# Attention and feed-forward layer on eight cores: the transposes that sum one tile's attention output are issued behind the output projection of the tile before it

## The chip, the cores and the metric

One Trainium2 chip, all eight NeuronCores, one launch. Each core computes 4096 of the 32768 rows on its own; no data goes between cores. The metric is device time in microseconds of the slowest core. Engines are named as in the profile: PE is TensorE (PEld its weight loads), DVE is VectorE, ACT is ScalarE, POOL is GpSimd, SP is SyncE, which here only issues DMAs.

## The reference, cut to what matters

The input is 4 x 8192 rows of 1024 float32. One layer is an attention in which each token attends only over its own 16 heads (a 16 x 16 score matrix for each token), and a gated feed-forward part with integer weights.

```python
Q = (x @ Wq.T).reshape(b, s, 16, 64)          # same for K, V; x is layer-normalised
scores = einsum('bshd,bstd->bsht', Q, K) / 8  # heads against heads, per token
attn = softmax(scores, axis=-1)
out = einsum('bsht,bstd->bshd', attn, V).reshape(b, s, 1024)
x = x + out @ Wfc.T
h = silu(ln(x) @ wg.T) * (ln(x) @ wu.T)       # hidden size 3072, weights int / 127
x = x + h @ wd.T
```

## The kernel before

The program has three stages with a barrier between them: the weights are transposed (to about 510 us), attention runs over 32 tiles of 128 tokens (about 480 to 2407 us), and the feed-forward part runs over 8 segments of 512 tokens (to the end). The change touches only the second stage.

A small class, `Sched`, keeps one list of instructions for each engine. Python code appends to the lists, so **the order of each engine's instructions is the order in which the code adds them**, and an engine runs its list strictly in that order. Waits are on counting semaphores.

The attention of a tile k is cut into pieces. In the main loop (step T from 0 to 35) each step adds one piece for each of several tiles:

- `front(T)` on DVE: four groups g, each a product of Q and K (L478, tile `gramB`, 128x4096), a folding add (L490, `gh`, 128x2048) and a sum (L502, `Ss`); then the maximum (L511) and the subtraction (L519, `Se`). ACT takes the exponential (L526).
- `a1(T-1)`: DVE normalises the scores (L535 to L554, tile `Aa`). Then POOL multiplies them with V in four groups g (L563, 128x4096 each), written to `avB[g % 2]`. So POOL can be two groups ahead of PE: group g waits (semaphore `aot`) until PE has read group g-2.
- `a2(T-2)`: PE adds up POOL's products with identity matmuls, 32 for each group, 128 in all, into `pOT` (L588). Each group waits for POOL's product of that group. ACT then copies `pOT` to the eight tiles `OT` (L604).
- `op2c(T-5)`: DVE applies the second layer norm (L383, `xn2m`), PE transposes it by eight matmuls (L671), ACT copies each (L680) and SP stores a finished block of four tiles.
- `op(T-3)`: PE multiplies `OT` with the output weights, twice eight matmuls (L622); DVE adds the residual to each half (L634, `x1p`); SP stores `x1p`; ACT sums values and squares (L345, L351).
- `op2m(T-4)`: four DVE instructions on 128x1 (L359, L362, L365, L367) and a logarithm and an exponential on ACT (L370, L375), for the second layer norm.
- `g_load(T+5)`, `g_a(T+4)`, `g_m(T+3)`: the load of a later tile, its sums on ACT and its own four DVE instructions of 128x1.
- `g_c(T+2)`: the first layer norm (L383, `xnm`), eight transposes (L425) with ACT copies (L433), and the 48 matmuls of Q, K and V (L452) with six copies by ACT (L466).

What sets the order around the change is only the order of these calls. POOL's list holds nothing but L563 in this stage, SP's the loads and stores. The two buffers of `avB` and the single `pOT` tie POOL and PE to each other:

```python
waits=[("amx", k + 1), ("aot", 4 * k + g - 1)], inc="apl")   # POOL, group g of tile k
w.append(("apl", 4 * k + g + 1))                              # PE, group g of tile k
```

Of the kernel before, what the change touches and what calls it, by code (L numbers as in the profile page):

```python
# [90 lines left out]
def build_program(taps=(), stop_after=None):  # L91
# [43 lines left out]
    with ExitStack() as TOP:  # L135
# [171 lines left out]
        with ExitStack() as ph:  # L307
# [268 lines left out]
            def back_a2(k):  # L576
                tt = k % 4
                for g in range(4):
                    for i in range(4):
                        for b in range(8):  # L580
                            w = []
                            if i == 0 and b == 0:
                                w.append(("apl", 4 * k + g + 1))
                                if g == 0:
                                    w.append(("aote", 8 * k))
                            S.add("tensor",
                                  lambda e, g=g, i=i, b=b:
                                  e.matmul(pOT[:, 128 * b:128 * (b + 1)],  # L588
                                           avB[g % 2][:, 1024 * i + 128 * b:
                                                       1024 * i + 128 * (b + 1)],  # L590
                                           ident[:],
                                           start=(g == 0 and i == 0
                                                  and b % 4 == 0),
                                           stop=(g == 3 and i == 3
                                                 and b % 4 == 3)),
                                  waits=w,
                                  inc=("aot" if (i == 3 and b == 7) else None))
                ev_w0 = [("aot", 4 * (k + 1))]
                if k - 4 >= 0:
                    ev_w0.append(("arp", 2 * (k - 4 + 1)))  # L600
                for b in range(8):
                    S.add("scalar",
                          lambda e, b=b, tt=tt:
                          e.copy(OT[b][:, tt * 128:(tt + 1) * 128],  # L604
                                 pOT[:, 128 * b:128 * (b + 1)]),
                          waits=(ev_w0 if b == 0 else []), inc="aote")
# [45 lines left out]
            def back_b2m(k):  # L652
                cap["l2m", k] = ln_mid(S, Lr2[k % 4], cap["l2a", k])
# [40 lines left out]
            def a1(k):  # L694
                if 0 <= k <= 31:
                    back_a(k)

            def a2(k):
                if 0 <= k <= 31:
                    back_a2(k)  # L700

            def op(k):
                if 0 <= k <= 31:
                    back_b(k)

            def op2m(k):
                if 0 <= k <= 31:
                    back_b2m(k)

            def op2c(k):  # L710
                if 0 <= k <= 31:
                    back_b2c(k)

            def g_load(k):
                if 5 <= k <= 31:
                    load_tile(k)

            def g_a(k):
                if 4 <= k <= 31:
                    ln1_a(k)  # L720

            def g_m(k):
                if 3 <= k <= 31:
                    ln1_m(k)

            def g_c(k):
                if 2 <= k <= 31:
                    ln1_c(k)
                    lnt(k)
                    proj(k)  # L730
# [11 lines left out]
            for T in range(36):  # L742
                if T <= 31:
                    front(T)
                a1(T - 1)
                a2(T - 2)
                op2c(T - 5)
                op(T - 3)
                op2m(T - 4)
                g_load(T + 5)  # L750
                g_a(T + 4)
                g_m(T + 3)
                g_c(T + 2)
# [175 lines left out]
```

How the kernel before makes its waits and increments, by code:

```python
                    def f(e):  # L71
                        for op in ops:
                            waits = list(op["waits"])
                            for tok in op["deps"]:
                                waits.append(selfcount[tok])
                            for (s, v) in waits:
                                key = (eng_name, s)
                                if v > 0 and hwm.get(key, 0) < v:
                                    e.wait_ge(sems[s], v)
                                    hwm[key] = v
                            ins = op["fn"](e)
                            if op["inc"] is not None:
                                ins.then_inc(sems[op["inc"]], op["incn"])
                            elif op["selfneed"]:
                                ins.then_inc(sems["sf" + eng_name], 1)
# [71 lines left out]
                    def f(e, k=k):  # L157
                        e.nop().then_inc(sems["ph"], 1)
                        e.wait_ge(sems["ph"], NENG * k)
# [7 lines left out]
                @blk.sync  # L167
                def _(sy):
                    t0 = cnt.get("tapd", 0)
                    add = [0]
                    def issue(dst, src):
                        sy.dma_start(dst, src).then_inc(sems["tapd"], 16)
                        add[0] += 16
                    for (_, fn) in todo:
                        fn(issue)
                    sy.wait_ge(sems["tapd"], t0 + add[0])
                    cnt["tapd"] = t0 + add[0]
```

## Time and profile before

| | us |
|---|---|
| median of the 2 runs shown (3659.9 and 3869.12) | 3764.51 |
| profiled execution, its own time | 3664.66 |
| its span, slowest core (core 0) | 3663.1 |
| spans of the eight cores | 3625.3 to 3663.1 |
| DVE busy | 1937.3 (53%) |
| PE busy | 2262.9 (62%) |
| POOL busy | 1138.4 (31%) |
| ACT busy | 682.4 (19%) |
| mean granted clock of TensorE, core 0 | 0.841 |

The span runs from the first to the last instruction of the slowest core. Busy shares are means over stages with different limits: in the attention stage DVE is the busiest engine, in the feed-forward stage PE is. A row of the timeline gives the start in us from the span's start, how long the instruction took in us, the engine, the line of the kernel, the operation with its output and inputs, and in square brackets the idle time in front of it with what ended it. An instruction that is held up after it was issued shows that as a longer duration, not as idle time.

### The profile page before, as it was taken

Reading aid. Unit: us, or ns where it says so; the run is one execution under the profiler, and the core shown is the slowest. Engines: PE = TensorE matmul, PEld = TensorE weight load, DVE = VectorE, ACT = ScalarE, POOL = GpSimd, SP = SyncE. Lnnn points to the kernel's source line nnn. Section 1 sums busy time; section 2 is a strip of 40 time slices with the busy share of each in tenths; the row PEclk is TensorE's granted clock in tenths of the full one; section 3 lists DMA queues with packets and bytes.
Section 4 is the critical chain, followed back from the end, with each engine's and each line's share of the span. In section 5 each row is a group of like instructions: output and inputs, shape, how many; then the busy total and the mean of one; then the engine's idle time right before and its main releaser. Section 6 shows DMA issues by size and latency. Waiting matters only on the chain. (4 is left out here: it accounts for less than half of the span.)

```text
span 3663.1 us, 38294 instructions; the slowest of 8 cores (3625.3 to 3663.1 us)
## 1 busy us (share of the span) xinstructions
PE 2262.9 (62%) x12192; PEld 1160.2 (32%) x12352; DVE 1937.3 (53%) x2305; ACT 682.4 (19%) x1691; POOL 1138.4 (31%) x447
## 2 busy tenths in 40 slices
PE   4433443554545555454555644468989889898897
PEld 2111112323333233333333333323434334343343
DVE  4433459988878787787878778511111111111111
ACT  0112231122222222122221211121101111011110
POOL 1000004546465554645446465601101111010110
PEclk9999996767777777777767766679999999999999
DMA  5445310000100101001010000034445444454443
GB/s 98 121 152 180 145 64 1 12 24 12 35 23 13 35 12 35 12 24 35 12 35 12 18 18 12 24 121 164 147 161 184 138 152 147 169 178 130 162 148 138
DMA packets 109631, 302.39 MB, mean 83 GB/s; under 512 B 13184, under 2 KB 29568, under 8 KB 108416
## 3 DMA queue, kind: packets, MB, share of 16 engines
q1 hardware_dynamic: 68736, 159.41, 13.4%
q0 software_dynamic: 32640, 121.65, 10.6%
q10 hardware_dynamic: 8064, 18.88, 1.3%
q8 instruction: 108, 1.77, 0.2%
q14 instruction: 83, 0.68, 0.1%
HBM read 247.46 MB, written 60.82 MB: 84 GB/s over the span
## 5 line engine op out<-in xcount | busy, mean ns | idle before, releaser
L563 POOL TENSOR_TENSOR avB<-Aa,Vs 128x4096 bf16<-128x4096 bf16 x128 | 971.3, 7608 | 1051.1 <-PE pOT L588 713.2
L588 PE MATMUL pOT<-ident,avB 128*128 128x128 bf16 x4096 | 344.9, 264 | 349.8 <-POOL avB L563 349.8
L834 DVE TENSOR_TENSOR hseg<-sg,pU 128x512 bf16<-128x512 bf16 x192 | 132.0, 688 | 620.4 <-PE pU L829 620.4
L588 PEld LDWEIGHTS pOT<-ident,avB 128*128 128x128 bf16 x4096 | 328.9, 121 | 368.9 <-issue 361.4
L815 PE MATMUL pG<-x2s,wgS 128*128 128x512 bf16 x1505 | 369.2, 387 | 44.2 <-DMA wgS<-d_wgT 40.6
L829 PE MATMUL pU<-x2s,wuS 128*128 128x512 bf16 x1505 | 366.8, 385 | 17.2 <-DMA wuS<-d_wuT 15.3
L270 PE MATMUL wps<-ident,wstg_b 128*128 128x128 bf16 x832 | 187.5, 265 | 285.8 <-ACT wstg_b L249 133.3
L861 PE MATMUL pD<-hseg,wdC 128*128 128x512 bf16 x1501 | 347.1, 386 | 18.5 <-DMA wdC<-d_wdT 14.6
L490 DVE TENSOR_TENSOR gh<-gramB 128x2048 bf16<-128x2048 bf16 x128 | 329.4, 2574 | 13.6 <-DVE gramB L478 0.5
L478 DVE TENSOR_TENSOR gramB<-Qs,Ks 128x4096 bf16<-128x4096 bf16 x128 | 319.4, 2495 | 25.5 <-ACT Vs L466 12.2
L804 POOL DMA_DIRECT2D wuS<-d_wuT x192 | 103.0, 537 | 727.3 <-PE pU L829 667.3
L502 DVE TENSOR_REDUCE Ss<-gh 128x64 f32<-128x2048 bf16 x128 | 292.6, 2286 | 13.2
L878 DVE TENSOR_TENSOR yst<-pT,x1s 128x128 f32<-128x128 f32 x256 | 63.6, 287 | 435.9 <-PE pT L871 435.6
L292 DVE CAST wpk<-wps 128x128 bf16<-128x128 f32 x576 | 143.0, 288 | 209.6 <-PE wps L270 207.8
L425 PE MATMUL pT<-ident,xnm 128*128 128x128 bf16 x256 | 53.1, 257 | 297.1 <-DVE xnm L383 211.6
L383 DVE TENSOR_SCALAR xn2m<-x1p,Lr 128x1024 bf16<-128x1024 f32 x32 | 222.7, 6958 | 12.9 <-ACT Lr L375 9.5
L820 ACT ACTIVATE sg<-pG 128x512 bf16<-128x512 f32 x192 | 114.6, 597 | 595.8 <-PE pG L815 595.7
L815 PEld LDWEIGHTS pG<-x2s,wgS 128*128 128x128 bf16 x1536 | 148.0, 99 | 236.5 <-issue 72.9
L829 PEld LDWEIGHTS pU<-x2s,wuS 128*128 128x128 bf16 x1536 | 151.4, 99 | 206.4 <-issue 33.2
L671 PE MATMUL pT<-ident,xn2m 128*128 128x128 bf16 x256 | 54.4, 271 | 259.1 <-DVE xn2m L383 223.6
L861 PEld LDWEIGHTS pD<-hseg,wdC 128*128 128x128 bf16 x1536 | 147.7, 99 | 196.1 <-issue 32.2
L270 PEld LDWEIGHTS wps<-ident,wstg_b 128*128 128x128 bf16 x832 | 86.6, 104 | 386.5 <-issue 354.6
(78 smaller groups left out, 2021.5 us busy)
## 6 DMA issues: line engine op xcount, KB each, us to landing
wuS<-d_wuT POOLq DMA_DIRECT2D x192, 256.0 KB, 3.2
wgS<-d_wgT SPq DMA_DIRECT2D x192, 256.0 KB, 2.7
wdC<-d_wdT POOLq DMA_DIRECT2D x64, 768.0 KB, 4.8
xcT<-x SPq DMA_DIRECT2D x32, 512.0 KB, 4.4
d_x<-x1p SPq DMA_DIRECT2D x32, 512.0 KB, 2.9
x1s<-d_x SPq DMA_DIRECT2D x8, 2048.0 KB, 13.7
y<-yst SPq DMA_DIRECT2D x32, 512.0 KB, 4.4
wstg_i<-wg SPq DMA_DIRECT2D x24, 512.0 KB, 3.6
```

The lines of the kernel that those rows point to most:

```text
L270: e.matmul(wps[b % 2][:, 0:128], wstg_b[j % 4][:, b * 128:(b + 1) * 128], ident[:], start=True, stop=True),
L292: e.tensor_copy(pdst(e), wps[b % 2][:, 0:128]),
L383: lambda e: e.tensor_scalar(out_fn(), xsrc_fn(), Lrt[:, 2:3], Lrt[:, 7:8], ALU.add, ALU.mult),
L478: e.tensor_tensor(gramB[g % 2][:].rearrange("p (t h d) -> p t h d", t=4, d=64), bass.AP(Qs[tt][:].tensor, Qs[tt][:].offset, [[1024, 128], ...
L490: e.tensor_tensor(gh1[:].rearrange("p (a b) -> p a b", b=32), bass.AP(gramB[g % 2][:].tensor, gramB[g % 2][:].offset, [[4096, 128], [64, 6 ...
L502: e.tensor_reduce(Ss[:, 64 * g:64 * (g + 1)] .rearrange("p (a b) -> p a b", b=1), gh1[:].rearrange("p (a b) -> p a b", b=32), AX.X, ALU.add),
L563: e.tensor_tensor(avB[g % 2][:].rearrange("p (t h d) -> p t h d", t=4, d=64), bass.AP(Aa[e4][:].tensor, Aa[e4][:].offset + 64 * g, [[256, ...
L588: e.matmul(pOT[:, 128 * b:128 * (b + 1)], avB[g % 2][:, 1024 * i + 128 * b: 1024 * i + 128 * (b + 1)], ident[:], start=(g == 0 and i == 0 ...
L815: e.matmul(pG[h % 2][:], wgS[h % 2][:, j * 128:(j + 1) * 128], x2buf[xp][j][:], start=(j == 0), stop=(j == 7)),
L829: e.matmul(pU[h % 2][:], wuS[h % 2][:, j * 128:(j + 1) * 128], x2buf[xp][j][:], start=(j == 0), stop=(j == 7)),
L834: lambda e, h=h: e.tensor_mul(hseg[h][:], sg[h % 2][:], pU[h % 2][:]),
L861: e.matmul(pD[c % 2][:], wdC[c % 2][:, k * 128:(k + 1) * 128], hseg[k][:], start=(k == 0), stop=(k == 23)),
```

## The change

Within each step of the main loop the call `a2(T - 2)` moves from ahead of `op2c(T - 5)` and `op(T - 3)` to behind them. Nothing else changes: the same instructions, buffers and semaphores.

```diff
                 a1(T - 1)
-                a2(T - 2)
                 op2c(T - 5)
                 op(T - 3)
+                a2(T - 2)
                 op2m(T - 4)
                 g_load(T + 5)
                 g_a(T + 4)
                 g_m(T + 3)
                 g_c(T + 2)
```

PE's list changes. Before, one step in the steady part, from the last matmuls of `g_c` to the first transposes of the next `g_c`:

```order
 L452 MATMUL pB<-WvJ,xnT 128x512 x8
 L588 MATMUL pOT<-ident,avB 128x128 x128
 L671 MATMUL pT<-ident,xn2m 128x128 x8
 L622 MATMUL pA<-WfJ,OT 128x512 x8
 L622 MATMUL pB<-WfJ,OT 128x512 x8
 L425 MATMUL pT<-ident,xnm 128x128 x8
```

The same place of PE's list after the change:

```order
 L452 MATMUL pB<-WvJ,xnT 128x512 x8
 L671 MATMUL pT<-ident,xn2m 128x128 x8
 L622 MATMUL pA<-WfJ,OT 128x512 x8
 L622 MATMUL pB<-WfJ,OT 128x512 x8
 L588 MATMUL pOT<-ident,avB 128x128 x128
 L425 MATMUL pT<-ident,xnm 128x128 x8
```

The 128 matmuls of `pOT` (L588) now stand behind the transposes of `xn2m` (L671) and the output projection (L622), and directly ahead of the transposes of `xnm` (L425).

ACT's list, one step in the steady part, as a difference (L604 is the copy of `pOT`, `Lr_1` a small tile of the second layer norm):

```order
 L466 CAST Vs<-pB 128x512
 L526 ACTIVATE Se<-Se 128x256
-L604 CAST OT<-pOT 128x128 x8
 L680 CAST xn2s<-pT 128x128 x8
 L345 ACTIVATE sqd,Lr_2<-x1p 128x1024
 L351 ACTIVATE sqd,Lr_2<-x1p 128x1024
+L604 CAST OT<-pOT 128x128 x8
 L370 ACTIVATE Lr_1<-Lr_1,c_eps 128x1
 L375 ACTIVATE Lr_1<-Lr_1 128x1
```

The eight copies of `pOT` follow the matmuls: they now stand behind the copies of `xn2s` and the two sums over `x1p`, and ahead of everything that belongs to `op2m`, `g_a`, `g_m` and `g_c`. The lists of DVE, POOL and SP are the same as before.

## Rows read from the trace of the kernel before

**Rows 1.** Stages: us, busy us (and count) of each engine, PE clock, DMA.

```profile
1200.00:1760.00 560.00, 304.56 (x1996) 181.00 (x2016) 451.30 (x311) 139.95 (x421) 287.23 (x39) 0.73 0.07 25
2560.00:3663.00 1103.00, 955.65 (x4230) 417.89 (x4316) 174.19 (x404) 134.23 (x226) 119.78 (x225) 0.98 0.46 155
```

**Rows 2.** Timeline of DVE through one step of the steady part.

```profile
1500.29 0.69 DVE L634 TENSOR_TENSOR x1p<-pB,xcT 128x512 f32<-128x512 f32 x1 [1.18 <-PE pB L622]
...
1504.11 2.29 DVE L478 TENSOR_TENSOR gramB<-Qs,Ks 128x4096 bf16<-128x4096 bf16 x1
...
1525.20 7.86 DVE L490 TENSOR_TENSOR gh<-gramB 128x2048 bf16<-128x2048 bf16 x1
...
1536.24 3.99 DVE L519 TENSOR_TENSOR Se<-Ss,Sm 128x256 bf16<-128x256 f32 x1
...
1542.60 7.67 DVE L383 TENSOR_SCALAR xn2m<-x1p,Lr 128x1024 bf16<-128x1024 f32 x1
1556.76 0.69 DVE L634 TENSOR_TENSOR x1p<-pA,xcT 128x512 f32<-128x512 f32 x1 [6.49 <-PE pA L622]
1558.48 0.69 DVE L634 TENSOR_TENSOR x1p<-pB,xcT 128x512 f32<-128x512 f32 x1 [1.03 <-PE pB L622]
```

**Rows 3.** Timeline of POOL through the same step (two instructions in each row).

```profile
1523.40 16.55 POOL L563 TENSOR_TENSOR avB<-Aa,Vs 128x4096 bf16<-128x4096 bf16 x2 [24.63 <-PE pOT L588]
1542.69 14.46 POOL L563 TENSOR_TENSOR avB<-Aa,Vs 128x4096 bf16<-128x4096 bf16 x2 [2.74 <-DVE Aa L554]
```

**Rows 4.** Timeline of PE through the same step.

```profile
1521.30 3.74 PE L588 MATMUL pOT<-ident,avB 128*128 128x128 bf16 x64
...
1540.10 3.28 PE L588 MATMUL pOT<-ident,avB 128*128 128x128 bf16 x32 [4.39 <-POOL avB L563]
1550.41 0.37 PE L671 MATMUL pT<-ident,xn2m 128*128 128x128 bf16 x2 [7.04 <-DVE xn2m L383]
```

**Rows 5.** DVE groups by line, whole span: count, duration ns min/median/max.

```profile
L490 DVE TENSOR_TENSOR gh<-gramB x128: 1224/1226/7865, 514.2 to 2293.7; 128x2048 bf16<-128x2048 bf16 x128
L519 DVE TENSOR_TENSOR Se<-Ss,Sm x32: 425/3990/3996, 537.0 to 2298.1; 128x256 bf16<-128x256 f32 x32
L383 DVE TENSOR_SCALAR xn2m<-x1p,Lr x32: 811/7673/7675, 786.9 to 2402.8; 128x1024 bf16<-128x1024 f32 x32
L502 DVE TENSOR_REDUCE Ss<-gh x128: 2285/2286/2289, 515.6 to 2295.0; 128x64 f32<-128x2048 bf16 x128
```

**Rows 6.** Timeline of DVE in step T = 3.

```profile
680.98 5.42 DVE L365 TENSOR_TENSOR Lr<-Lr 128x1 f32<-128x1 f32 x1
686.50 6.88 DVE L367 TENSOR_TENSOR Lr<-Lr 128x1 f32<-128x1 f32 x1
```

**Rows 7.** Timeline of POOL in step T = 3.

```profile
679.36 14.02 POOL L563 TENSOR_TENSOR avB<-Aa,Vs 128x4096 bf16<-128x4096 bf16 x2 [7.15 <-DVE Aa L554]
```

**Rows 8.** Timeline of DVE where step T = 30 ends.

```profile
2257.57 0.69 DVE L634 TENSOR_TENSOR x1p<-pB,xcT 128x512 f32<-128x512 f32 x1 [1.66 <-PE pB L622]
...
2259.41 9.16 DVE L478 TENSOR_TENSOR gramB<-Qs,Ks 128x4096 bf16<-128x4096 bf16 x1
```

**Rows 9.** Timeline of PE, then of POOL, at the same place.

```profile
2257.29 3.74 PE L588 MATMUL pOT<-ident,avB 128*128 128x128 bf16 x64
...
2259.39 16.06 POOL L563 TENSOR_TENSOR avB<-Aa,Vs 128x4096 bf16<-128x4096 bf16 x2 [3.79 <-PE pOT L588]
```

**Rows 10.** Timeline of DVE: second residual add of steps 5 and 31.

```profile
803.43 0.69 DVE L634 TENSOR_TENSOR x1p<-pB,xcT 128x512 f32<-128x512 f32 x1 [1.71 <-PE pB L622]
...
2316.62 0.69 DVE L634 TENSOR_TENSOR x1p<-pB,xcT 128x512 f32<-128x512 f32 x1 [0.97 <-PE pB L622]
```

**Rows 11.** Timeline of all engines in the stage's last steps.

```profile
2384.05 0.81 DVE L383 TENSOR_SCALAR xn2m<-x1p,Lr 128x1024 bf16<-128x1024 f32 x1 [2.02 <-ACT Lr L375]
...
2394.01 0.69 DVE L634 TENSOR_TENSOR x1p<-pB,xcT 128x512 f32<-128x512 f32 x1 [1.75 <-PE pB L622]
...
2406.57 0.43 ACT L680 CAST xn2s<-pT 128x128 bf16<-128x128 f32 x2 [0.33 <-PE pT L671]
```

## The prediction, made before the changed kernel ran

> **What bounds the kernel now.** I read the stage table first. The change lies in the attention stage, where DVE is busy 451 of 560 us and PE only 305, at a granted clock of 0.73; in the feed-forward stage PE is busy 956 of 1103 us at 0.98, and that stage holds none of the moved instructions, so I leave it as it is [rows 1]. So DVE's list sets the pace of the stage, and the question is what DVE does in its 58 us per step.
>
> The timeline of DVE through one step, from one second residual add to the next, is 1500.29 to 1558.48 us: 58.2 us [rows 2]. Two things in it are not DVE's own work:
>
> - It stands idle twice for the output projection, 6.49 and 1.03 us, 7.5 in all [rows 2].
> - Three of its instructions are far longer than the shortest of their kind: L490 7.86 instead of 1.22, L519 3.99 instead of 0.42, L383 7.67 instead of 0.81 [rows 2, 5]. That is 6.6 + 3.6 + 6.9 = 17.1 us.
>
> POOL's timeline beside it says why. POOL multiplies at 1523.40 to 1539.95 and at 1542.69 to 1557.15, two instructions each time [rows 3]. L490 starts at 1525.20, behind the start of a POOL instruction, and ends about when that one does; L519 and L383 are caught in the same way. The sum L502 never stretches: its 128 executions lie between 2285 and 2289 ns, many beside POOL [rows 5]. Even instructions of one element are caught: L365 takes 5.42 and L367 6.88 us while POOL runs its two from 679.36 on [rows 6, 7]. So in this kernel a POOL product of some 7.0 us (14.02 for two) shuts out these elementwise instructions of DVE until it ends; then DVE gets one through, and then POOL's next one runs. The sums pass, and so do the adds from PSUM (L634, 0.69 us at 1556.76, where POOL is still busy). The Trainium skill says as much for part of these (GPSIMD Engine Reference, Key points: GpSimd shares its SBUF interfaces with VectorE and contends with its two-input and two-port instructions); the stretched L490 and L365 have two inputs, so the trace agrees.
>
> The own work of DVE is then 58.2 - 7.5 - 17.1 = 33.6 us per step, and the step is decided by **where POOL's four products (28 us) fall in DVE's list**.
>
> **The change part by part.**
>
> *PE's order.* What could be gained is the wait of the adds for the output projection, now 7.5 us. But PE was not late because of L588: its last group starts at 1540.10 and takes 3.28, so it is over at 1543.4, and PE then idles 7.04 us for xn2m [rows 4]. From the end of xn2m (1550.27) to the end of the second add (1559.17) there are 8.9 us of transposes and projection, which the change leaves in a row. So the gain here is nothing in the steady part.
>
> *When POOL may start.* POOL's third group of a tile waits for PE to have read the first. Before, PE reads it at 1521.30, right behind the projections, in the middle of DVE's front; two groups run there, and the first two groups of the next tile run behind Aa at 1542.69, the second of them beside the 7.5 us in which DVE is idle anyway [rows 2 to 4]. That idle time is where POOL was free of charge. After the change PE comes to L588 only when the output projection is over, which is at the second add. The end of step 30 shows this meeting by chance, because PE was late there: L588 starts at 2257.29, the second add at 2257.57, POOL at 2259.39 [rows 8, 9]. So POOL's third group will start 1.8 us behind the start of the second add, or 1.0 us behind its end. By then Aa of the next tile is long made, and PE frees each buffer in 3.3 to 3.7 us, within the 7 us of the next product. **All four products will run back to back right behind the second add.**
>
> *The walk.* Let 0 be the end of the second add. DVE's list then holds eight instructions of one element, 0.26 us apart, of which the third, fourth, seventh and eighth have two inputs; then xnm at 2.1 and L478 at 3.0 (as 1500.99 to 1504.11 [rows 2]).
>
> - POOL's first, 1.0 to 8.0: L365 of the second group of four, issued at 1.6, is held to about 8.2. By the nearest row L365 loses 5.3 us issued later in a product; here 6.5.
> - POOL's second, to 15.1: L367 is held, 6.88 instead of 0.16 [rows 6]: 6.7.
> - POOL's third, to 22.1: xnm is held as xn2m is now, 7.67 instead of 0.81 [rows 5]: 6.9.
> - POOL's fourth, to 29.6: L478 is held, 9.16 instead of 2.29, as at 2259.41 [rows 2, 8]: 6.9.
>
> That is 27.0 us held instead of 17.1: +9.9 us a step. Nothing else in the step is then held, since POOL is through by 30 us; xn2m is free, but the 7.5 us idle stay behind it. The step becomes 33.6 + 7.5 + 27.0 = 68.1 us.
>
> *Other engines.* PE's list: behind L588 stand the transposes of xnm and Q, K, V. L588 ends about 19 us into the step, xnm is there at 23, and the 48 matmuls end near 39; the front that needs them starts more than 25 us later. Covered; without that cover it would cost 20 us a step. ACT: the eight copies of pOT now hold L370 and L375, g_a and the copies of g_c till about 21 us; their users on DVE come at 58 us or in the next step. SP's and POOL's lists don't change; SP's loads wait for the adds of tiles seven back, so they don't matter.
>
> *The clock.* PE will idle some 20 us ahead of the transposes, not 7. Where they start behind other work, end of xn2m to end of the second add is 8.9 us; in the stage's last steps, with few matmuls around, it is 2384.86 to 2394.70, 9.8 us [rows 2, 11]. I take the upper one: +0.9 a step, bounds 0 and 0.9.
>
> *How many steps.* From step 5 to step 31 the second add goes from 803.43 to 2316.62, 26 steps of 58.2 us [rows 10]. Each gets +9.9 + 0.9: 26 x 10.8 = +281.
>
> *The start.* In steps 3 and 4 there is no op2c, so the projection goes ahead without a wait: step 4 loses an idle time that I take as half of the steady 7.5 us, 4. In step 5 POOL's last two groups move to behind the add, so this step is held by no product: about -17. Small shifts in steps 3 and 4 give 2 more: together -23.
>
> *The tail.* From the second add of step 31 (over at 2317.3) to the end of the stage (2407.0) it is 90 us [rows 10, 11]. After the change POOL has ten products left there instead of eight, at 7 us with PE's reads between the last of them, and each of PE's pieces waits its turn: my walk gives 111 us, +21 (bounds 0 and 40).
>
> Sum: 281 - 23 + 21 = +279, on the profiled execution's own 3664.7: **3944 us, 7.6% slower.** I say 3940. The median of the runs shown, 3764.5, is of two that lie 209 us apart; the profiled one agrees with the lower, and I add to that.
>
> **The rivals.**
>
> 1. *POOL's burst falls a little later.* If L588 starts later or on a slow clock, POOL's first product starts when L478 has begun. Then L490, L478, L490 and L478 are hit, and two of the four holds are cut by L502, which runs beside POOL (2.3 us each): about 22.6 us held, +5.5 and +0.9 a step. 26 x 6.4 = +166, with start and tail +164: 3829. For it: step 30 was only 1.0 us from there. Against it: the row of L588 has 64 matmuls in 3.74, fast, behind a projection [rows 9].
> 2. *No change.* The products slip into the idle time as now. For this POOL would have to start two of them 30 us later, with Aa ready; nothing holds it back. 3665.
> 3. *Faster: holds need a two-port mode.* If only xnm and xn2m could be held and the other three stretched kinds have another cause tied to the old places, a step would be 33.6 + 7.5 + 6.9 + 0.9 = 48.9, 9.3 less than now, over 26 steps -242: 3423. It decides from the point that no two-input instruction is held. Against it stand L365, L367 and L478, held in other places [rows 6, 8]. The Trainium skill speaks for it: Advanced Engine Details and Errata, VectorE Performance Modes, names only two-port instructions as those that GpSimd blocks. L490 and L365 say otherwise here.
> 4. *Much slower.* The Q, K, V path becomes late because ACT and PE stand behind L588. It needs 25 us that I don't see; +5 a step more would give 4070.
>
> **How the numbers follow.** Forecast 0.70, rival 1 0.15, rival 4 0.07, rival 2 0.05, rival 3 0.03. About 2% either way is what a measurement of this kernel tells from no change; faster 0.03, same 0.05, slower 0.92. The range goes from between rival 1 and the forecast to just short of rival 4, 3840 to 4050; its upper part also takes in that the runs shown scatter upwards.
>
> **What would show it.** Right: a DVE step of 68 us; L365, L367, xnm and the first L478 at 6.6 to 9.2 us each step, L490, L519 and xn2m back at 1.2, 0.42 and 0.81; POOL in one burst of four behind the second add; the adds still waiting 6 to 7 us for PE. Wrong: stretched instructions elsewhere, products beside DVE's idle time, or DVE idle ahead of L478 for ACT's copies of Q and K.

## The result, and the profile after

The changed kernel takes 1.069 times as long as the kernel before (95% interval 1.0647 to 1.0733): 3910 to 3941 us against 3657 to 3696. The profiled execution took 3913.5 us, against 3664.7 before, so +249; 3940 was forecast. Nearly every kernel here also had executions some 1 to 7% longer, with a lower TensorE clock on one die or both; all times and ratios below leave these out.

The stages of the changed kernel (core 5, its slowest; us, busy us of PE, PEld, DVE, ACT and POOL, clock, DMA share, GB/s):

```profile
1200.00:1760.00 560.00, 270.22 (x1732) 159.70 (x1732) 468.46 (x260) 118.12 (x362) 244.70 (x36) 0.68 0.06 19
2680.00:3780.00 1100.00, 971.07 (x4346) 421.67 (x4345) 175.03 (x397) 136.64 (x230) 122.26 (x229) 0.98 0.48 157
```

Against [rows 1], DVE is busier in the attention stage, 468 us instead of 451, although it got through fewer instructions, 260 instead of 311, and POOL did 36 products instead of 39. More busy and less done is the sign of an instruction that waits after it was issued. The feed-forward stage is as it was.

The timeline of DVE from one second add of the output projection on:

```profile
1598.53 0.69 DVE L634 TENSOR_TENSOR x1p<-pB,xcT 128x512 f32<-128x512 f32 x1 [1.85 <-PE pB L622]
...
1599.85 0.16 DVE L365 TENSOR_TENSOR Lr<-Lr 128x1 f32<-128x1 f32 x1
1600.12 0.16 DVE L367 TENSOR_TENSOR Lr<-Lr 128x1 f32<-128x1 f32 x1
1600.38 0.15 DVE L359 TENSOR_SCALAR Lr<-Lr 128x1 f32<-128x1 f32 x1
1600.64 0.15 DVE L362 TENSOR_SCALAR Lr<-Lr 128x1 f32<-128x1 f32 x1
1600.90 6.50 DVE L365 TENSOR_TENSOR Lr<-Lr 128x1 f32<-128x1 f32 x1
1607.51 6.88 DVE L367 TENSOR_TENSOR Lr<-Lr 128x1 f32<-128x1 f32 x1
1614.50 7.41 DVE L383 TENSOR_SCALAR xnm<-xcT,Lr 128x1024 bf16<-128x1024 f32 x1
1622.01 8.93 DVE L478 TENSOR_TENSOR gramB<-Qs,Ks 128x4096 bf16<-128x4096 bf16 x1
```

POOL in the same stretch:

```profile
1600.36 28.43 POOL L563 TENSOR_TENSOR avB<-Aa,Vs 128x4096 bf16<-128x4096 bf16 x4 [39.73 <-PE pOT L588]
```

And PE:

```profile
1589.38 0.37 PE L671 MATMUL pT<-ident,xn2m 128*128 128x128 bf16 x2 [18.40 <-DVE xn2m L383]
...
1592.24 3.57 PE L622 MATMUL pA<-WfJ,OT 128*128 128x512 bf16 x8
1595.61 2.82 PE L622 MATMUL pB<-WfJ,OT 128*128 128x512 bf16 x8
1598.26 3.74 PE L588 MATMUL pOT<-ident,avB 128*128 128x128 bf16 x64
```

Read them together. PE reaches L588 at 1598.26, at the second add (1598.53). The first 32 of these 64 matmuls free a buffer, and POOL starts at 1600.36, 1.1 us behind the end of the add. Its four products then run in one piece for 28.4 us, where before they came in two pairs [rows 3]. Each catches one instruction of DVE: a pair of instructions on a single element, 6.50 and 6.88 us long instead of 0.16, then xnm, then the first L478. The instructions that were held before are free now:

```profile
L490 DVE TENSOR_TENSOR gh<-gramB x128: 1224/1226/7864, 516.0 to 2523.3; 128x2048 bf16<-128x2048 bf16 x128
...
L519 DVE TENSOR_TENSOR Se<-Ss,Sm x32: 425/425/4032, 538.8 to 2527.7; 128x256 bf16<-128x256 f32 x32
...
L383 DVE TENSOR_SCALAR xnm<-xcT,Lr x32: 812/7412/7554, 495.2 to 2413.5; 128x1024 bf16<-128x1024 f32 x32
L383 DVE TENSOR_SCALAR xn2m<-x1p,Lr x32: 811/812/1504, 773.7 to 2652.4; 128x1024 bf16<-128x1024 f32 x32
```

These groups by line give minimum, median and maximum in ns. The median of L519 fell from 3990 to 425 and that of xn2m from 7673 to 812, while xnm rose to 7412; compare [rows 5].

Where the 249 us came from, by the second adds of steps 5 and 31 and the last copy of the stage:

```profile
783.19 0.69 DVE L634 TENSOR_TENSOR x1p<-pB,xcT 128x512 f32<-128x512 f32 x1 [1.42 <-PE pB L622]
...
2540.60 0.69 DVE L634 TENSOR_TENSOR x1p<-pB,xcT 128x512 f32<-128x512 f32 x1 [1.86 <-PE pB L622]
...
2656.10 0.54 ACT L680 CAST xn2s<-pT 128x128 bf16<-128x128 f32 x2 [0.23 <-PE pT L671]
```

Up to step 5 the changed kernel is 20.2 us ahead (783.2 against 803.4); over the next 26 steps it loses 244.2 (1757.4 us against 1513.2); behind step 31 it loses 25.7 more (115.3 against 89.7, from the add's end to the end of the stage). The sum, 249.7, is the whole difference of the two profiled executions (248.8), to within a microsecond.

For all kernels, the 26 steps from the second add of step 5 to that of step 31 split as follows. "Held" is the time by which DVE's instructions were longer than the shortest of their kind (0.16 us for L365 and L367 in either form), "idle" the gaps between them beyond the 0.1 us that lies between any two. Both are summed from the trace of the slowest core (for e5_split2 core 2, for e10_all_new_order core 5) and divided by 26; us per step:

| kernel | step | held | of it, mainly | idle |
|---|---|---|---|---|
| before | 58.2 | 17.2 | xn2m 6.9, L490 5.6, L519 3.3 | 7.7 |
| changed | 67.6 | 26.1 | L478 7.0, xnm 6.4, L367 6.2, L365 5.8 | 8.1 |
| e1_single | 64.9 | 23.3 | L478 10.9, L490 6.9, xnm 5.3 | 8.2 |
| e2_before4 | 58.5 | 17.6 | xn2m 6.9, L367 6.7, L365 4.0 | 7.6 |
| e3_after4 | 67.6 | 26.1 | as changed | 8.1 |
| e4_moved | 61.3 | 21.8 | L490 13.3, L478 8.5 | 6.3 |
| e5_split2 | 54.1 | 13.2 | xn2m 3.3, L490 3.2, L544 2.9, L541 2.2 | 7.5 |
| e6_small_idle | 55.0 | 16.6 | xn2m 6.9, L541 4.9, L519 3.5 | 5.1 |
| e8_old_late_pool | 67.1 | 26.1 | L367 12.9, L365 12.1 | 7.7 |
| e9_all | 52.4 | 13.7 | L383 4.5, L490 3.0, L544 2.9, L541 2.2 | 5.3 |
| e10_all_new_order | 53.8 | 15.7 | L490 12.8, L478 2.5 | 4.8 |
| e11_split4 | 53.0 | 8.8 | L383 1.9, L544, L547 and L554 1.5 each | 10.9 |

### The profile page after: what moved, and what is told of

Same layout as the page of the kernel before. It is cut to its first block and busy times, and to the rows that moved or that the text cites. A ratio compares the mean times of both kernels' runs of the same rounds, so it can differ in the third digit from the quotient of the medians.

```text
span 3911.9 us, 38454 instructions; the slowest of 8 cores (3883.2 to 3911.9 us)
## 1 busy us (share of the span) xinstructions
PE 2313.1 (59%) x12352; PEld 1166.9 (30%) x12352; DVE 2155.3 (55%) x2305; ACT 683.8 (17%) x1691; POOL 1085.5 (28%) x447
## 3 DMA queue, kind: packets, MB, share of 16 engines
q1 hardware_dynamic: 68736, 159.41, 12.8%
## 5 line engine op out<-in xcount | busy, mean ns | idle before, releaser
L563 POOL TENSOR_TENSOR avB<-Aa,Vs 128x4096 bf16<-128x4096 bf16 x128 | 918.3, 7204 | 1365.7 <-PE pOT L588 1130.5
L588 PE MATMUL pOT<-ident,avB 128*128 128x128 bf16 x4096 | 344.4, 263 | 293.0 <-POOL avB L563 293.0
L478 DVE TENSOR_TENSOR gramB<-Qs,Ks 128x4096 bf16<-128x4096 bf16 x128 | 480.4, 3753 | 27.0 <-ACT Vs L466 13.7
L588 PEld LDWEIGHTS pOT<-ident,avB 128*128 128x128 bf16 x4096 | 328.1, 121 | 312.2 <-issue 304.7
L671 PE MATMUL pT<-ident,xn2m 128*128 128x128 bf16 x256 | 55.4, 270 | 577.9 <-DVE xn2m L383 544.0
L861 PE MATMUL pD<-hseg,wdC 128*128 128x512 bf16 x1536 | 352.4, 387 | 18.6 <-DMA wdC<-d_wdT 17.2
L502 DVE TENSOR_REDUCE Ss<-gh 128x64 f32<-128x2048 bf16 x128 | 292.6, 2286 | 13.2
L671 PEld LDWEIGHTS pT<-ident,xn2m 128*128 128x128 bf16 x256 | 25.0, 105 | 616.9 <-issue 611.4
L425 PE MATMUL pT<-ident,xnm 128*128 128x128 bf16 x256 | 54.6, 265 | 252.3 <-DVE xnm L383 207.9
L367 DVE TENSOR_TENSOR Lr<-Lr 128x1 f32<-128x1 f32 x64 | 198.4, 3100 | 6.9 <-DVE Lr L365 0.3
```

Source lines behind the costliest of these rows:

```text
L367: Sch.add("vector", lambda e: e.tensor_sub(Lrt[:, 5:6], Lrt[:, 3:4], Lrt[:, 4:5]), chain=True, inc="aln")
L478: e.tensor_tensor(gramB[g % 2][:].rearrange("p (t h d) -> p t h d", t=4, d=64), bass.AP(Qs[tt][:].tensor, Qs[tt][:].offset, [[1024, 128], ...
L502: e.tensor_reduce(Ss[:, 64 * g:64 * (g + 1)] .rearrange("p (a b) -> p a b", b=1), gh1[:].rearrange("p (a b) -> p a b", b=32), AX.X, ALU.add),
L563: e.tensor_tensor(avB[g % 2][:].rearrange("p (t h d) -> p t h d", t=4, d=64), bass.AP(Aa[e4][:].tensor, Aa[e4][:].offset + 64 * g, [[256, ...
L588: e.matmul(pOT[:, 128 * b:128 * (b + 1)], avB[g % 2][:, 1024 * i + 128 * b: 1024 * i + 128 * (b + 1)], ident[:], start=(g == 0 and i == 0 ...
L861: e.matmul(pD[c % 2][:], wdC[c % 2][:, k * 128:(k + 1) * 128], hseg[k][:], start=(k == 0), stop=(k == 23)),
```

## The experiments

The theory was that POOL's product shuts out certain instructions of DVE while it runs, and that the change costs time because it moves POOL's four products behind the second add. The rival was that PE's and ACT's new order costs the time by itself, by delaying what is queued behind L588 and its copies.

### Four buffers of avB in the old order and in the new (e2_before4, e3_after4)

```diff
-            Vs = [... for t in range(8)]
+            Vs = [... for t in range(4)]
-            avB = [... for i in range(2)]
+            avB = [... for i in range(4)]
...
-                          waits=[("amx", k + 1), ("aot", 4 * k + g - 1)],
+                          waits=[("amx", k + 1), ("aot", 4 * k + g - 3)],
```

The room comes from Vs, four instead of eight, and from one gramB instead of two. The second kernel has the change on top. Expected of the first:

> Old order, four buffers of avB instead of two, so that POOL no longer waits for PE inside a tile (the room comes from one gramB instead of two and four Vs instead of eight). Theory (POOL's products shut out DVE's two-input instructions, and the change costs time because it puts all four behind the second add): all four products now start right behind Aa in either order. Held: xn2m 6.9, one L365 about 4.5, one L367 6.7, some 18 us; idle 7.6; step about 59 us, total about 3690 us (3665 to 3720). Rival (the change costs time because L588 and its copies delay the pieces behind them on PE and ACT, and the stretched DVE instructions only reflect that): 3660, as before, since the old order is kept.

Expected of the second:

> New order, with the same four buffers. Theory: the order on PE no longer decides when POOL runs, so this equals the old order with four buffers within 1%: about 3690 us, step about 59 us, held instructions xn2m, L365, L367. Rival: the order on PE and ACT is what costs, so the 6.9% stay: about 3915 us, step 68 us.

Measured: 1.0023 (0.9982 to 1.0065) times the kernel before, 3674 us, for the old order; 3917 us twice for the new. The first time lies between the two expectations, 3690 and 3660, so it decides nothing, but the held instructions are the ones that the theory named. The second is a miss of mine: 3690 was expected, and it came out at the rival's 3915. What POOL waited for (us in total, times) shows why. Old order, four buffers:

```profile
L563 POOL TENSOR_TENSOR avB<-Aa,Vs x128: 7018/7026/7479, 569.6 to 2368.8; 128x4096 bf16<-128x4096 bf16 x128
its engine sat idle before it (us, times) until:
  DVE Aa L554: 1122.7, 32
```

New order, four buffers:

```profile
L563 POOL TENSOR_TENSOR avB<-Aa,Vs x128: 7023/7031/9076, 566.7 to 2622.2; 128x4096 bf16<-128x4096 bf16 x128
its engine sat idle before it (us, times) until:
  PE pOT L588: 1062.1, 28
```

Four buffers hold one tile. In the new order they are all still full with the tile before when Aa is ready, since PE reads them only behind the projection. So POOL waited for PE as ever and ran its burst at the same place. The edit did not undo what it was to undo, and the two times tell nothing between theory and rival. An experiment the other way round was needed.

### The old order, with POOL made late (e8_old_late_pool)

On top of e2_before4:

```diff
-                          waits=[("amx", k + 1), ("aot", 4 * k + g - 3)],
+                          waits=[("amx", k + 1), ("aot", 4 * k + g - 3),
+                                 ("arev", 2 * (k - 1))],
```

> Old order on every engine, four buffers of avB, and one wait more: POOL's products of tile k also wait for the residual adds of tile k-2, the second add of the step. PE's and ACT's order are those of before. Theory: this puts POOL's burst of four where the change put it, so the cost of the change must appear without the change: held L365 6.3, L367 6.7, xnm 6.6, L478 6.6, step about 68 us, total about 3915 us (3885 to 3935). Rival (PE and ACT order cost the time): at most the 1 to 2 us of a step by which a burst is longer, under 3720.

Measured: 3921 and 3938 us, against 3663 to 3683 for the kernel before beside them and 3674 for e2_before4. PE, ACT and DVE have exactly the order of the kernel before, and the whole cost of the change is there. DVE, then POOL and PE (here L635 is the residual add):

```profile
1410.18 0.69 DVE L635 TENSOR_TENSOR x1p<-pB,xcT 128x512 f32<-128x512 f32 x1 [0.96 <-PE pB L623]
...
1411.50 6.56 DVE L365 TENSOR_TENSOR Lr<-Lr 128x1 f32<-128x1 f32 x1
1418.17 6.88 DVE L367 TENSOR_TENSOR Lr<-Lr 128x1 f32<-128x1 f32 x1
1425.67 6.36 DVE L365 TENSOR_TENSOR Lr<-Lr 128x1 f32<-128x1 f32 x1
1432.14 6.88 DVE L367 TENSOR_TENSOR Lr<-Lr 128x1 f32<-128x1 f32 x1
1439.12 0.81 DVE L383 TENSOR_SCALAR xnm<-xcT,Lr 128x1024 bf16<-128x1024 f32 x1
```

```profile
1411.02 27.98 POOL L563 TENSOR_TENSOR avB<-Aa,Vs 128x4096 bf16<-128x4096 bf16 x4 [38.33 <-DVE x1p L635]
...
1440.19 0.39 PE L425 MATMUL pT<-ident,xnm 128*128 128x128 bf16 x2 [30.12 <-DVE xnm L383]
```

POOL starts here 0.15 us behind the add, not 1.1 us, so the holds fall on other instructions than expected: on four instructions of one element, and xnm passes free. Four instructions with 0.6 us of work between them take 26.7 us, and the step is 67.1 us, against 67.6 in the changed kernel: the plainest form of the effect. PE runs nothing in the 30.12 us before 1440.19, through the whole burst, so its matmuls do not hold DVE either. The rival falls: the order of PE and ACT is not needed for the cost, only the place of the burst.

### One input instead of two (e1_single)

The changed kernel, with the two instructions of one element written differently:

```diff
-                Sch.add("vector", lambda e: e.tensor_mul(
-                    Lrt[:, 4:5], Lrt[:, 2:3], Lrt[:, 2:3]), chain=True)
+                Sch.add("vector", lambda e: e.tensor_scalar(
+                    Lrt[:, 4:5], Lrt[:, 2:3], Lrt[:, 2:3], None, ALU.mult), chain=True)
```

and L367 likewise.

> Changed kernel, with L365 and L367 (products and differences of one element) written as instructions with one input tile and a per-partition scalar, as L359 is with one input. Theory: they are no longer held, and the four products meet xnm (held 5.9 instead of 6.6, it is issued 1 us into the first), L478 6.7, L490 6.6 and, behind L502, L478 4.6: 23.8 us held instead of 26.2, step 65.7 instead of 68.1, total about 3855 us (3840 to 3875). Rival A (any instruction of DVE that small is held): no change, 3915. Rival B (PE and ACT order): no change, 3915.

Measured: 3841 us, ratio 1.0488 (1.0472 to 1.0505) to the kernel before; 3855 was expected. DVE beside a burst of POOL that begins at 1431.41:

```profile
1432.06 0.21 DVE L365 TENSOR_SCALAR Lr<-Lr 128x1 f32<-128x1 f32 x1
1432.39 0.21 DVE L367 TENSOR_SCALAR Lr<-Lr 128x1 f32<-128x1 f32 x1
1432.71 6.28 DVE L383 TENSOR_SCALAR xnm<-xcT,Lr 128x1024 bf16<-128x1024 f32 x1
1439.09 8.93 DVE L478 TENSOR_TENSOR gramB<-Qs,Ks 128x4096 bf16<-128x4096 bf16 x1
1448.12 7.87 DVE L490 TENSOR_TENSOR gh<-gramB 128x2048 bf16<-128x2048 bf16 x1
1456.09 2.29 DVE L502 TENSOR_REDUCE Ss<-gh 128x64 f32<-128x2048 bf16 x1
1458.48 6.54 DVE L478 TENSOR_TENSOR gramB<-Qs,Ks 128x4096 bf16<-128x4096 bf16 x1
```

The same arithmetic on the same element passes in 0.21 us beside a running product once it reads only one input and a scalar. The holds move on to the next instructions of the list, in the expected order, and the second L478 loses only 4.25 us because the sum L502 ran beside the product first.

### The small instructions into the idle time (e4_moved)

The changed kernel, with the eight small instructions of a step ahead of the projection:

```diff
                 op2c(T - 5)
+                op2m(T - 4)
+                g_m(T + 3)
                 op(T - 3)
                 a2(T - 2)
-                op2m(T - 4)
                 g_load(T + 5)
                 g_a(T + 4)
-                g_m(T + 3)
```

> Changed kernel, with op2m and g_m (the eight small DVE instructions and their logarithms and exponentials on ACT) called ahead of the output projection, so that DVE runs them in its idle time. Theory: idle time 8.4 falls to 6.3; behind the second add DVE comes to L478 just as POOL starts, so the holds are L490 6.6, L478 4.6, L490 6.6, L478 4.6 (22.4) or begin with L478 6.7 (24.5): step 62.2 to 64.3, total 3765 to 3820 us. Rival (PE and ACT order): only the 2.1 us of idle time are filled, step 66, total 3862 us.

Measured: 3746 to 3754 us, ratio 1.0241 (1.0224 to 1.0257) to the kernel before, a little under the expected range, which began at 3765. Idle time went from 8.1 to 6.3, as it should. POOL starts at 1404.56 here and finds L478 in the way:

```profile
1404.45 2.29 DVE L478 TENSOR_TENSOR gramB<-Qs,Ks 128x4096 bf16<-128x4096 bf16 x1
1406.85 7.86 DVE L490 TENSOR_TENSOR gh<-gramB 128x2048 bf16<-128x2048 bf16 x1
1414.81 2.29 DVE L502 TENSOR_REDUCE Ss<-gh 128x64 f32<-128x2048 bf16 x1
1417.20 6.54 DVE L478 TENSOR_TENSOR gramB<-Qs,Ks 128x4096 bf16<-128x4096 bf16 x1
1423.85 7.86 DVE L490 TENSOR_TENSOR gh<-gramB 128x2048 bf16<-128x2048 bf16 x1
```

This is the prediction's first rival, made to happen by an edit: if the burst meets DVE's front part, two of its four holds are shortened by L502, and the step costs 21.8 us of holds instead of 26.1. Moving 2 us of work thus gave 6.3 us a step. POOL's four products took 34.04 us here instead of 28.4, as each of them also waited for the DVE instruction then running or let through.

### Shorter products, and fast versions (e5_split2, e6_small_idle, e9_all)

Kernel before, with each product in two halves of 128x2048 (t=2 instead of t=4):

```diff
                 for g in range(4):
-                    S.add("gpsimd", ...)
+                    for u in range(2):
+                        S.add("gpsimd", ...)
```

> Kernel before, each product of POOL cut into two of half the size. Theory: one hold lasts at most one POOL instruction, so 3.5 us instead of 7.0, and more of POOL's time lies beside L502, L511 and DVE's idle time: held L490 3.4, L519 0.5, L541 2.6, L544 3.3, xn2m 3.4, L365 about 1, 14.2 us instead of 17.0, step 55.3 instead of 58.1, total about 3585 us (3560 to 3610). Rival (DVE slows down by a share of POOL's time, whatever the length of its instructions): no change, 3660 us.

Measured: 3534 and 3551 us, ratio 0.964 (0.9587 to 0.9693) to the kernel before. A hold is as long as what is left of one POOL instruction, so the length of POOL's instructions matters by itself, though POOL's whole work is the same. The gain was larger than the 2% expected and the times lie below the stated range: step 54.1 us instead of 55.3.

Kernel before, with the edits of e1_single and e4_moved:

> Kernel before, with L365 and L367 as instructions with one input, and op2m and g_m called ahead of the output projection. Theory: POOL's fourth product runs beside DVE's idle time there, and these eight instructions with one input pass beside it, so 2.1 us of work fall into idle time: step 56.0 instead of 58.1, total about 3602 us (3590 to 3620). Rival (they are held there like others): xn2m and one of them wait for the fourth product, nothing is gained, 3660 us.

Measured: 3573 to 3600 us, ratio 0.9761 (0.9711 to 0.9811): faster, though the interval leaves open whether by 2%. In the step from 1405.20 the eight small instructions take 0.15 to 0.21 us each at 1451.96 to 1454.17, beside POOL's fourth product (1451.3 to 1458.7), in time that was idle. Not foreseen was that POOL's first pair of a step now holds L519 and L541, where it held L490 and L519.

Both edits together on the kernel before:

> Kernel before with both edits: products of half size, and the eight small instructions with one input ahead of the projection. Theory: the two add up, held 13.2, idle 5.5, step 52.2 us, total about 3500 us (3475 to 3530). Rival: they share a gain, about 3560 us.

Measured: 3481 us, a single time (spans of 3445 to 3480 us on the eight cores), 5% below the kernel before. The step is 52.4 us, with 52.2 expected. Of the 13.7 us still held there, 5.5 are in Aa's chain, L541 to L547, and 4.5 in L383 (DVE, beside products of 3.6 us):

```profile
1379.14 2.51 DVE L541 TENSOR_TENSOR Sm<-Sl,Sr 128x16 f32<-128x16 f32 x1
1381.76 3.46 DVE L544 TENSOR_SCALAR Sm<-Sm 128x16 f32<-128x16 f32 x1
1385.33 3.46 DVE L547 TENSOR_TENSOR Sr<-Sr,Sm 128x16 f32<-128x16 f32 x1
...
1389.42 4.25 DVE L383 TENSOR_SCALAR xn2m<-x1p,Lr 128x1024 bf16<-128x1024 f32 x1
```

### The change again, on the fast version (e10_all_new_order)

```diff
-                a2(T - 2)
                 op2c(T - 5)
                 op2m(T - 4)
                 g_m(T + 3)
                 op(T - 3)
+                a2(T - 2)
```

> Both edits of the fastest kernel so far, in the order of the change. Theory: a hold is at most one POOL instruction of 3.5 us, and in the front part every second one is mostly covered by L502. Eight of them in one burst behind the second add hold L490 3.3 and L478 1.2 in turn, some 17.5 us; idle 6.3; step 57.3 us instead of 52 in the old order; total about 3625 us (3600 to 3650), so the change still costs, but half of what it did (4% instead of 6.9%). Rival (the change costs by PE's and ACT's order, the length of POOL's instructions only adds to it): the full 250 us on top of 3481, 3730 us.

Measured: 3510 to 3516 us, ratio 0.9593 (0.9575 to 0.9612) against the kernel before, so some 30 us or 0.8% above e9_all's single time, which comes from another chip. The step is 53.8 us against 52.4. The theory's direction holds and the rival's 3730 is far off, but the size is a miss: 3625 was expected. DVE behind the second add (L636):

```profile
1354.43 0.69 DVE L636 TENSOR_TENSOR x1p<-pB,xcT 128x512 f32<-128x512 f32 x1 [1.55 <-PE pB L624]
...
1358.54 4.44 DVE L490 TENSOR_TENSOR gh<-gramB 128x2048 bf16<-128x2048 bf16 x1
1363.09 2.29 DVE L502 TENSOR_REDUCE Ss<-gh 128x64 f32<-128x2048 bf16 x1
1365.48 3.12 DVE L478 TENSOR_TENSOR gramB<-Qs,Ks 128x4096 bf16<-128x4096 bf16 x1
```

A pair of half products costs 3.2 us at L490 and 0.8 at L478, as L502 covers more of the second one than I had taken; four such pairs make nearly all of the 15.7 us held. Idle time is 4.8 instead of 6.3. From the end of xn2m to the end of the second add it is 8.5 us in the mean, against 9.8 in e4_moved, and PE stands idle 2.2 us ahead of these transposes, behind the 48 matmuls of Q, K and V, against 11.7. I had not looked at that neighbour. That the shorter pause is the reason is not shown: e9_all has 2.2 us of it as well and takes 9.1.

### Quarter products (e11_split4)

The fastest version in the old order, with `range(4)` and t=1.

> The fastest kernel so far in the old order, with each product cut into four instead of two. Theory: the holds get shorter again, but POOL's third and fourth groups then decide when PE is through with L588, and with it the transposes behind, at nearly the time that xn2m sets now; so DVE's holds turn into idle time: 3480 us, within 1%. Rival (holds alone count): held about 8 us instead of 13, step 47 us, total about 3350 us.

Measured: 3472 and 3475 us, against the single time of 3481 for the halves: no difference that these runs can show. Holds fell to 8.8 us and idle time rose to 10.9. PE, and then DVE's first add, show where it went:

```profile
1390.84 3.57 PE L590 MATMUL pOT<-ident,avB 128*128 128x128 bf16 x32 [4.47 <-POOL avB L564]
1394.20 0.40 PE L673 MATMUL pT<-ident,xn2m 128*128 128x128 bf16 x2
...
1401.68 0.69 DVE L636 TENSOR_TENSOR x1p<-pA,xcT 128x512 f32<-128x512 f32 x1 [10.42 <-PE pA L624]
```

DVE is through with xn2m at 1388.94, but PE still waits for POOL's last group (L590 here) and comes to its transposes (L673) only at 1394.20. The hold was not the last limit; behind it stands the chain from POOL through L588 to the projection.

## Why the prediction was right

- **What bounds the kernel.** Right. DVE sets the step, and its own work was the same before and after, 33.3 to 33.4 us (step less held less idle), with 33.6 forecast.
- **Nothing gained at the adds.** Right. The first add still waits 6 to 7 us for PE after xn2m; the changed kernel's idle time is 8.1 us a step, not less than 7.7.
- **POOL's burst behind the second add, 1.0 us behind its end.** Right: 1.1 us in the row above, all four products in one piece.
- **The walk of the four holds.** Right by instruction: L365 and L367 of the second set, xnm, L478. Forecast 6.5, 6.7, 6.9 and 6.9; in the step shown 6.3, 6.7, 6.6 and 6.6.
- **The clock, +0.9.** Half right, and sized from a single step. Idle time rose by 0.4 us a step. From the end of xn2m to the end of the second add it was 10.0 us in the step shown, with 3.57 and 2.82 us for the projection's two times eight matmuls, and 9.8 was forecast. But over the 26 steps the mean went from 9.2 to 9.7 only: the 8.9 that I started from lay below the mean, and in three of the changed kernel's steps the projection took 3.0 and 1.9 us, and the step 66.5.
- **The number of steps.** The term was sized a little too high: +281 forecast, +244 measured, 9.4 us a step instead of 10.8. The holds in full steps are 26.3 us instead of 27.0, as those of xnm and L478 were priced 0.3 too high each; half of the clock's 0.9 did not come; and the last two of the 26 steps, 64.8 and 64.2 us, no longer have the second set of small instructions. I had priced all 26 alike.
- **Start and tail.** -23 forecast and -20 measured; +21 forecast and +26 measured.
- **The rivals.** The burst that falls later was real as a mechanism (e4_moved), but not in this kernel. The third rival decided from the point that no two-input instruction is held; L365 is held with two inputs and free with one (e1_single), which rules that out. For the other elementwise instructions only their holds are shown, not what in them is needed for it. That nothing changes did not happen either: POOL stood idle through DVE's waits for the projection. That Q, K, V become late did not happen; DVE never waited for them in the steady part.

That this is the cause, and not a companion of it, rests above all on e8_old_late_pool, which has the cost without the new order, and on e10_all_new_order, where the new order costs 1.4 us a step (against e9_all) instead of 9.4. e4_moved says less: it lies 3.1 us a step above the kernel before, but e6_small_idle, with the same move and the edit of e1_single in the old order, is itself 3.2 us below it.

## What to carry to other kernels

Read a DVE group's minimum beside its median: where the median is many times the minimum, the instruction is being held, and the timeline of POOL tells by what. In this kernel what a POOL product costs depends on what DVE has next in its list, so ask of any reordering on a third engine when it will let POOL start, and what DVE is doing then. Here cutting POOL's instructions in halves gained 3.6%, and cutting them in quarters on top of the other edits nothing more; its work cost least where DVE reduces, reads PSUM or is idle.

## What the runs showed of the hardware that was not expected

The length of a hold does not depend on the size of the held instruction: in the changed kernel one of one element a partition (L367) waited 6.7 us, and one of 128x1024 (L383) 6.6. Whether it is held does depend on the form: L365 with two input tiles is held, and with one input and a per-partition scalar it passes in 0.21 us (e1_single). One input alone is no safe pass, however: L544, one input of 128x16 with constants, was held 3.3 us (3.46 against 0.17) in e9_all, and L383, one input of 128x1024 with per-partition scalars, 6.6 us in the changed kernel. So of the TENSOR_SCALARs here those of one element pass (L359 and L362 in 0.15 us too) and the larger ones are held, while the sums (L502, 2.29 us) and the reciprocal of 128x16 (L540, 0.25 us in e9_all) pass at any size seen. What decides this no run isolates.

The hold works both ways. POOL's product takes 7.02 us at its shortest, but 9.07 us in e4_moved, where it was issued 0.11 us behind the start of an L478 of 2.29 us. The two products of [rows 3] that take 16.55 us together, 8.6 and 8.0, met DVE instructions in the same way.

Cutting POOL's 128x4096 product (7.0 us) into halves and quarters made little extra work: 3.60 us at the shortest for a half and 1.89 for a quarter, so 7.2 and 7.5 us for the whole.
